# Order of the first attention's steps and of the gate constants in a two-layer kernel, one core

## The chip, the cores and the metric

The kernel runs on one core of a Trainium2 chip. It is one launch: every input is copied in from HBM, six blocks are computed one after the other, and the output is stored. The metric is the device time of one execution in microseconds (us). The engines of the core work through queues of their own, in the order in which the program wrote them, and wait for each other by semaphores: TensorE (PE), VectorE (DVE), ScalarE (ACT), GpSimd (POOL) and SyncE (SP), which here only issues DMAs.

## The reference

`x` is 4 x 128 tokens of width 128, `ctx` is 4 x 2048 x 128. Six blocks follow each other, each as `x = x + block(layernorm(x))`. The change touches the first and the fourth, and the hand-over from the first to the second.

```python
# block 1: cross attention with a mask; 16 heads of 8 channels
Q = heads(x @ Wq.T + bq); K = heads(ctx @ Wk.T + bk); V = heads(ctx @ Wv.T + bv)
scores = einsum('bhqd,bhkd->bhqk', Q, K) / sqrt(8)
scores = where((kidx - head) % 16 != 0, -inf, scores)     # head h sees keys h, h+16, ... : 128 keys
out = softmax(scores) @ V;  return out @ Wo.T + bo
# block 2: selective state space (x @ W_in, a causal convolution of 4 taps, silu, delta, scan, gate, W_out)
# block 3: SwiGLU with quantised weights and activations
# block 4: gated attention
gate = ctx @ Wg + bg
attn = softmax(einsum('bkd,bqd->bkq', gate, x), axis=1)    # over the 2048 keys
out = einsum('bkq,bkd->bqd', attn, ctx);  return out @ Wo + bo
# block 5: self attention with a relative bias; block 6: an 8-bit MLP
```

In block 4 the kernel never forms `gate`: it multiplies the queries by `Wg` ("gated queries", `g_T`) and adds, for each query, the product with `bg` (the gate constant, `c_gate`), which is one number per token. The softmax then needs a shift per token: minus the largest score of its row, with the constant taken in.

## The kernel before

**The tiling.** A batch is a tile of 128 tokens, there are four. In the first attention a head sees 128 keys, so a batch has 16 score tiles of 128 x 128; they are worked in four *groups* of four heads, one group to a PSUM bank (512 columns). Sixteen groups in all, numbered `w` or `t`.

**One group's way.** `scores` (PE): products of depth 32, since a group's four heads share a strip of 32 rows of `q_heads` and of the keys. `maximum_of` (DVE, L889): the row maxima from PSUM. `difference` (DVE, L897): scores minus maximum to `diff`. `turn_diff` (PE, L1402): four transposes back into the same bank. `exponentials` (ACT, L578): to `probs_T`, two batches deep.

**One batch's way.** `keys_values` (PE) and the copies of ACT (L550) give keys and values; `turn_values` (PE, L1345) turns the values and DVE (L843, `keys_values`) places them. `heads` (PE) multiplies the probabilities of four groups with the values, and with ones for the sums; `inverse` (ACT, L584 and L588) makes 1/sum; `scaled` (DVE, L884) gives `attn_T`; the projection (PE) goes to bank 5; `add` (DVE, L952) and `moments` give `x` and its statistics; `rsqrt_var` (ACT, L536), `normed` (DVE, L823), `turn_xn` (PE, L1316) and `copy_xn_T` (ACT, L544) give the turned, normalised input of block 2. Its convolution and gates are `channels(i, part)` on PE, by `SSM_GROUPS` (batches 0 and 1 together, then 2, then 3), then the product with `w_x` (`dbc_ps`), which the whole state-space block waits for.

**What sets the order.** Each engine has a loop over steps `t` (`attention(ph)`, ph 0 for the first attention, ph 1 for the self attention); a step's work is due at `t = stage + 4b` by the numbers in the line `VALUES, SCALE, ...`, the same for each batch. In phase 0 `scores` is called for every second `t` with two *strips* (two groups at a time, two banks), on a ring of five banks; in phase 1 it is called with four strips at once. The step `t` of PE is: scores, values, two `turn_diff`, `heads`, keys, projection, `turn_xn`, channels.

**Weights.** ACT makes sums of absolute weights at t = 6, 7, 8 (L605, the first waits for the DMA of `late_sb`); PE adds them up (`weight_sums`) in bank 7, DVE reads them (L853 to L855) at t = 10. The maxima of two more weights (L849), `pair_of_maxima`, `weight_maxima`, `spread_maxima` and `weight_inverses` stand at t = 16 to 22.

**Fills.** `keep_warm(n, bank)` is n matmuls of `ones` without a use, put where PE would stand still.

**The gated block.** Per batch: `turn_xn`, `copy_xn_T`, `gated_queries` (PE), `copy_g` (ACT, L731), four `gated_scores` of 512 keys, `maximum` (DVE, L1164), `shifts` (L1168 to L1171), the exponentials (ACT, L754, with `shift` as bias), transposes (L1723), copies (L1204), `mix`. The first batches run between the last steps of block 3: `turn_hidden` (L1631), its copy (L714) and `down` for batches 2 and 3.

## Time and profile before

| what | us |
|---|---|
| median of 3 runs (lowest, highest) | 236.3 (236.25, 237.12) |
| the profiled execution, its own time | 236.94 |
| its span, first to last instruction | 235.1 |
| PE busy / DVE busy / ACT busy / POOL busy in the span | 200.7 / 172.6 / 119.7 / 88.3 |
| mean granted TensorE clock | 0.977 |
| first attention and hand-over (first scores to the product that block 2 waits for) | 10.0 to 62.1 |
| block 2 and block 3 | 62.1 to 133 |
| gated block | 133 to 178 |
| self attention, MLP, store | 178 to 235.1 |

The time of a run is that of the whole execution, the span is what the profiler saw between its first and last instruction; 1.84 us lie around it. Times inside the profile count from the start of the span. The profiled execution lies within the runs shown, 0.64 above their median.

### The profile page before, as it was taken

The numbers are of one execution on the slowest core, as the hardware profiler recorded it, in microseconds if no ns is written. First come the engines' busy times: TensorE is split into PE (matmuls) and PEld (weight loads), VectorE is DVE, ScalarE is ACT, GpSimd is POOL, SyncE is SP. The second block draws the span as 40 slices with busy tenths as digits, with TensorE's granted clock in tenths as the row PEclk, the third lists the DMA queues.
The fourth block names the chain that finished last, engine by engine and source line by source line (L and its number), as shares of the span: only waits on it lengthen the run. The fifth ranks groups of instructions, "written<-read, shape, count | busy, mean of one in ns | idle before, by whom it ended". The sixth has DMA issues, their size and how long they took to land.

```text
span 235.1 us, 5061 instructions
## 1 busy us (share of the span) xinstructions
PE 200.7 (85%) x1868; PEld 141.3 (60%) x1868; DVE 172.6 (73%) x486; ACT 119.7 (51%) x292; POOL 88.3 (38%) x104
## 2 busy tenths in 40 slices
PE   8879998799997799999986679999988798876832
PEld 5568777688663245454463446867885776664421
DVE  2489485733399999999789879497775868816785
ACT  3343633435878897986065636335242344453431
POOL 7002408110047799998423064400002566522000
PEclk9999999999999999999999999999999999997696
DMA  6999950000079988300000001400000000000001
GB/s 213 389 427 409 418 242 4 3 0 0 8 216 377 233 96 96 56 1 0 0 3 0 0 0 50 133 0 3 0 0 3 0 4 3 3 3 3 0 0 45
DMA packets 9224, 20.23 MB, mean 86 GB/s; under 512 B 736, under 2 KB 5472, under 8 KB 8176
## 3 DMA queue, kind: packets, MB, share of 16 engines
q1 hardware_dynamic: 8912, 19.78, 27.2%
q8 instruction: 15, 0.25, 0.4%
q10 hardware_dynamic: 288, 0.13, 0.2%
q14 instruction: 9, 0.07, 0.1%
HBM read 17.52 MB, written 2.38 MB: 85 GB/s over the span
## 4 chain that ended last, share of the span: by engine, by line
PE 39%; POOL 17%; DVE 16%; issue 16%; ACT 7%; DMA 3%; SPq 1%; POOLq 0%; DVEq 0%; ACTq 0%
PE bank L1299 32%; POOL region L496 9%; POOL diff L520 6%; DMA ctx_T_sb<-ctx_T 3%; PE bank L1723 3%; PE bank L1402 2%; DVE diff L897 1%; DVE ext L1260 1%; DVE ext L1261 1%; DVE neg_max L889 1%; DVE region L1275 1%; PE bank L1316 1%; ACT region L676 1%; POOL region L485 1%; DVE region L1129 1%
## 5 line engine op out<-in xcount | busy, mean ns | idle before, releaser
L1054 DVE TENSOR_TENSOR_SCAN region<-region,bank 128x512 f32<-128x512 f32 x32 | 37.1, 1203 | 0.9 <-ACT region L690 0.8
L1299 PE MATMUL bank<-region,early_sb 128*128 128x512 f32 x64 | 33.8, 621 | 3.2 <-POOL region L496 2.1
L578 ACT ACTIVATE region<-bank 128x512 f32<-128x512 f32 x32 | 18.6, 594 | 21.7 <-PE bank L1402 21.5
L1299 PE MATMUL bank<-ones 128*128 128x256 bf16 x198 | 28.5, 300 | 1.1 <-POOL ones L432 1.0
L1299 PEld LDWEIGHTS bank<-ones 128*128 128x128 bf16 x198 | 20.6, 107 | 8.0 <-issue 2.2
L536 ACT ACTIVATE lnv<-mv,eps_col 128x1 f32<-128x1 f32 x24 | 7.0, 291 | 31.6 <-DVE mv L819 21.2
L690 ACT ACTIVATE region<-region,a_neg 128x508 f32<-128x508 f32 x32 | 21.1, 708 | 2.3 <-DVE region L1054 1.2
L1402 PE MATMUL bank<-early_sb,diff 128*128 128x128 f32 x128 | 18.8, 280 | 3.8 <-POOL diff L520 3.2
L1299 PE MATMUL bank<-ctx_T_sb,region 128*32 128x128 f32 (+1 forms) x160 | 20.7, 341 | 1.1 <-DMA ctx_T_sb<-ctx_T 0.7
L520 POOL TENSOR_TENSOR diff<-region,neg_max 128x512 f32<-128x512 f32 x15 | 15.5, 1044 | 12.4 <-DVE neg_max L908 12.4
L453 POOL TENSOR_TENSOR xb<-x,rows_sb 128x512 f32<-128x512 f32 x3 | 3.8, 1266 | 39.0 <-DVE x L1179 27.9
L1299 PEld LDWEIGHTS bank<-region,early_sb 128*128 128x128 f32 x64 | 9.8, 189 | 13.8 <-POOL region L496 13.0
L1402 PEld LDWEIGHTS bank<-early_sb,diff 128*128 128x128 f32 x128 | 14.0, 141 | 6.7 <-POOL diff L520 4.1
L908 DVE CUSTOM_DVE_ANT_0 region<-bank,region 128x128 f32<-128x128 f32 x64 | 14.4, 286 | 3.6 <-PE bank L1299 3.6
L1299 PE MATMUL bank<-k_T,region 32*128 32x128 f32 x256 | 15.1, 283 | 2.2 <-ACT k_T L550 1.0
L676 ACT ACTIVATE region<-region,b_tok 128x256 f32<-128x256 f32 x36 | 15.3, 495 | 2.5 <-PE bank L1576 2.5
L1299 PEld LDWEIGHTS bank<-region,ctx_sb 128*128 128x128 f32 x128 | 15.2, 192 | 1.9 <-issue 1.9
L1299 PEld LDWEIGHTS bank<-k_T,region 32*128 32x128 f32 x256 | 12.7, 186 | 5.3 <-ACT k_T L592 1.7
L1204 DVE COPY region<-bank 128x512 f32<-128x512 f32 x16 | 10.9, 686 | 6.6 <-PE bank L1723 6.5
L1299 PE MATMUL bank<-region,ctx_sb 128*128 128x128 f32 x128 | 15.6, 275 | 0.0
L1576 PEld LDWEIGHTS bank<-early_sb,region 128*128 128x128 f32 x72 | 9.0, 141 | 9.1 <-issue 8.1
L889 DVE TENSOR_REDUCE neg_max<-bank 128x4 f32<-128x512 f32 x16 | 10.3, 684 | 3.5 <-PE bank L1299 3.5
(234 smaller groups left out, 412.1 us busy)
## 6 DMA issues: line engine op xcount, KB each, us to landing
ctx_sb<-ctx SPq DMA_DIRECT2D x4, 1024.0 KB, 23.9
ctx_T_sb<-ctx_T SPq DMA_DIRECT2D x3, 1024.0 KB, 10.3
late_sb<-late SPq DMA_DIRECT2D x1, 2416.0 KB, 17.3
bias_scratch<-bias_vec SPq DMA_DIRECT2D x1, 2040.0 KB, 25.3
ctx_T_sb<-ctx_T SPq DMA_DIRECT2D x2, 512.0 KB, 5.9
diff<-c_scratch SPq DMA_DIRECT2D x4, 256.0 KB, 6.2
x<-c_scratch SPq DMA_DIRECT2D x4, 256.0 KB, 6.4
region<-bias_scratch SPq DMA_DIRECT2D x1, 1024.0 KB, 5.6
```

Source lines behind the costliest of these rows:

```text
L496: done(pool.tensor_tensor(read[:, k % 3, :], state[:, k % 3, :], c_rows(n), ALU.mult), "read")
L520: done(pool.tensor_tensor(diff[:, w % 4], neg_biased[:, t % 3], neg_max[:, w % 4, :, None].to_broadcast([P, HG, P]), ALU.subtract), "diff")
L578: done(act.activation(probs_T[:, w % (2 * NG)].rearrange("p h q -> p (h q)"), step_bank(w)[:, :], ACT.Exp, scale=1.0 if w < 16 else -1.0), ...
L676: ins = act.activation(du_B[:, i % 2, b].rearrange("p h c -> p (h c)"), du_T[:, b].rearrange("p h c -> p (h c)"), ACT.Copy, scale=b_tok[:, ...
L690: done(act.activation(dst, src, ACT.Exp, scale=a_neg[:, hf, n:n + 1]), "decay")
L889: done(dve.tensor_reduce(neg_max[:, w % 4, :], step_bank(w)[:, :].rearrange("p (h k) -> p h k", h=HG), AX, ALU.max, negate=True), "neg_max")
L908: ins = dve.tensor_tensor_reduce(neg_biased[:, t % 3, j, :], src[:, j, :], rel_bias[:, HG * g + j, :], -1.0, HIGHEST, ALU.add, ALU.min, ne ...
L1054: done(dve.tensor_tensor_scan(state[:, k % 3, :], decay[:, k % NDA, :], bank[3 + k % 3][:, :], 0.0, ALU.mult, ALU.add), "state")
L1204: done(dve.tensor_copy(p2_T[:, w % 4].rearrange("p c q -> p (c q)"), bank[4 + w % 2][:, :]), "p2T_sb")
L1299: return pe.matmul(dst, lhsT, rhs, start=start, stop=stop)
L1402: ins = pe.transpose(step_bank(w)[:, j * P:j * P + P], diff[:, w % 4, j, :], ident)
L1576: ins = pe.transpose(bank[3 + k % 3][:, b * P:b * P + P], du_B[:, BY_PE.index(n) % 2, b, hf, :], ident)
```

## The change

It has two parts.

**The first attention.** `scores` of phase 0 is called four times with four strips, once per batch: at t = 0, and then at t = 3, 7 and 11 behind `heads`. The ring of five banks gives way to a list of banks, and the wait on `probs_T_sb` is set so that two of the four groups' banks are free of older exponentials. A table `FIRST` gives for each step of a batch its own t in phase 0 (phase 1 keeps the old numbers). PE's loop ends at t = 17; the last `heads`, the last projection, the four `turn_xn` and all `channels` stand behind it in an order written out. The fills ahead of `heads` are left out for batches 2 and 3. The sums of weights move from bank 7 at t = 9 to bank 6 at t = 13 (PE) and from t = 10 to t = 15 (DVE); the maxima move behind DVE's loop. ACT's copies of the keys stand one step earlier, ahead of the exponentials of that step. The turned tiles of the first layer norm all go to bank 7, so that each `turn_xn` waits for the copy of the tile before; those of block 2's norm go to bank 6.

**The gated block.** The gate constants are made for batch 0 alone, for batch 1 alone, and for 2 and 3 together, where they were made by pairs. PE makes those of batch 0 ahead of the first scores, and turns batch 1 behind all four scores of batch 0 where it stood between the second and the third. DVE's `shifts` is a reduction with the sign turned and one operation with two steps, where it was a reduction and two operations.

On PE around the third batch's `heads` (names: `k_T` are scores, `diff` are `turn_diff`, `v_heads` and `ones_heads` are `heads`, `attn_T` the projection, `ones` a fill). Before:

```order
38 L1402 MATMUL bank<-early_sb,diff 128x128 x4
39 L1299 MATMUL bank<-cols_sb,attn_T 128x128
40 L1299 MATMUL bank<-k_T,region 128x128 x8
41 L1345 MATMUL bank<-early_sb,k_T 128x128 x2
42 L1402 MATMUL bank<-early_sb,diff 128x128 x8
43 L1299 MATMUL bank<-k_T,region 128x128 x8
44 L1402 MATMUL bank<-early_sb,diff 128x128 x4
45 L1299 MATMUL bank<-ones 128x256 x6
46 L1299 MATMUL bank<-region,v_heads 32x128 x16
```

On PE, the same place after:

```order
33 L1305 MATMUL bank<-k_T,region 128x128 x16
34 L1305 MATMUL bank<-cols_sb,attn_T 128x128
35 L1353 MATMUL bank<-early_sb,k_T 128x128 x2
36 L1410 MATMUL bank<-early_sb,diff 128x128 x8
37 L1305 MATMUL bank<-w_red,ones 128x3
38 L1305 MATMUL bank<-late_sb 16x256
39 L1410 MATMUL bank<-early_sb,diff 128x128 x4
40 L1305 MATMUL bank<-region,v_heads 32x128 x16
41 L1305 MATMUL bank<-region,ones_heads 32x128 x16
42 L1410 MATMUL bank<-early_sb,diff 128x128 x12
43 L1305 MATMUL bank<-cols_sb,attn_T 128x128
44 L1324 MATMUL bank<-early_sb,xn 128x128
```

All scores of batch 3 now stand ahead of the projection of batch 1 and of the last transposes, the sums of weights stand between them, the fill is gone, and three groups are turned behind `heads` of batch 2.

On PE at the hand-over (`region 128x256` and `128x128` are the convolutions, `region,late_sb` 256 or 128 wide are gates, 104 rows high is the product that block 2 waits for; `w_diag` is `spread_maxima`). Before:

```order
52 L1299 MATMUL bank<-region 128x256 x4
53 L1299 MATMUL bank<-ones 128x256 x6
54 L1299 MATMUL bank<-region,v_heads 32x128 x16
55 L1299 MATMUL bank<-region,ones_heads 32x128 x16
56 L1316 MATMUL bank<-early_sb,xn 128x128
57 L1299 MATMUL bank<-region 128x256 x4
58 L1299 MATMUL bank<-cols_sb,attn_T 128x128
59 L1299 MATMUL bank<-region,late_sb 128x256 x2
60 L1299 MATMUL bank<-region 128x128 x8
61 L1299 MATMUL bank<-region,late_sb 128x128 x2
```

On PE, the same place after:

```order
45 L1305 MATMUL bank<-region,v_heads 32x128 x16
46 L1305 MATMUL bank<-region,ones_heads 32x128 x16
47 L1324 MATMUL bank<-early_sb,xn 128x128
48 L1305 MATMUL bank<-region 128x256 x4
49 L1324 MATMUL bank<-early_sb,xn 128x128
50 L1305 MATMUL bank<-cols_sb,attn_T 128x128
51 L1305 MATMUL bank<-region 128x256 x4
52 L1324 MATMUL bank<-early_sb,xn 128x128
53 L1305 MATMUL bank<-region 128x128 x8
54 L1305 MATMUL bank<-region,late_sb 128x256 x2
55 L1305 MATMUL bank<-region,late_sb 128x128 x2
```

The first convolution, which stood ahead of the last `heads`, now stands behind it, and `spread_maxima`, once followed by eight convolutions and a gate, is now (four rows on, beyond this piece) the last thing ahead of the 104-high product.

On PE at the start of the gated block (`cols_sb,xn_T` are the gate constants, `ctx_T_sb` the scores, `ident_b` is `turn_hidden`). Before:

```order
140 L1316 MATMUL bank<-early_sb,xn 128x128
141 L1299 MATMUL bank<-xn_T,late_sb 128x128
142 L1299 MATMUL bank<-ctx_T_sb,region 128x512 x2
143 L1316 MATMUL bank<-early_sb,xn 128x128
144 L1299 MATMUL bank<-ctx_T_sb,region 128x512 x2
145 L1299 MATMUL bank<-xn_T,late_sb 128x128
146 L1299 MATMUL bank<-cols_sb,xn_T 128x1 x2
147 L1631 MATMUL bank<-ident_b,region 128x128 x4
```

On PE, the same place after:

```order
134 L1324 MATMUL bank<-early_sb,xn 128x128
135 L1305 MATMUL bank<-xn_T,late_sb 128x128
136 L1305 MATMUL bank<-cols_sb,xn_T 128x1
137 L1305 MATMUL bank<-ctx_T_sb,region 128x512 x4
138 L1324 MATMUL bank<-early_sb,xn 128x128
139 L1305 MATMUL bank<-xn_T,late_sb 128x128
140 L1305 MATMUL bank<-cols_sb,xn_T 128x1
141 L1650 MATMUL bank<-ident_b,region 128x128 x4
```

The transpose of batch 1, and all that follows from it, moved from the middle of the scores to their end.

The diff, cut to what the text speaks of:

```diff
-RING = 5
 VALUES, SCALE, PROJECT, ADD, RSTD, NORM, TURN = 6, 7, 7, 8, 8, 9, 10
 BY_HAND = 2
 
+FIRST_BANKS = (0, 1, 2, 3, 4, 7, 0, 1, 2, 3, 4, 7, 1, 0, 2, 3)
...
+FIRST = {"heads": {7: 0, 11: 1, 14: 2}, "inverse": {7: 0, 11: 1, 15: 2, 18: 3}, "scale": {7: 0, 11: 1, 15: 2, 19: 3},
+         "project": {7: 0, 11: 1, 17: 2}, "add": {8: 0, 12: 1, 16: 2, 20: 3}, "moments": {8: 0, 14: 1, 16: 2, 20: 3},
+         "rstd": {8: 0, 17: 1, 19: 2, 20: 3}, "norm": {9: 0, 15: 1, 19: 2, 21: 3}, "turned": {17: 0, 18: 1, 19: 2, 21: 3}}
...
+def batch_at(ph, t, what):
+
+    if ph == 0:
+        return FIRST[what].get(t)
+    b = due(t, LATER[what])
+    return b if b is None or what in ("heads", "inverse", "scale") or b < BY_HAND else None
...
-SSM_GROUPS = [(0, 2, [(1, 0), (1, 2 * P)], (0, 0)), (2, 3, [(2, 0), (2, P)], (2, 2 * P)),
+SSM_GROUPS = [(0, 2, [(1, 0), (1, 2 * P)], (0, 0)), (2, 3, [(2, 0), (2, P)], (7, 2 * P)),
...
-            at = bank[[7 - b % 2 * 4, 7, 5 + b % 2, 7 if b == 3 else b][n]]
+            at = bank[[7, 6, 5 + b % 2, 7 if b == 3 else b][n]]
...
-                    if ph == 0 and t % NG == 3 and t // NG + 1 < NB:
+                    if ph == 0 and t % NG == 2 and t // NG + 1 < NB:
...
-                    if ph == 0 and t == WEIGHTS + 4:
+                            token_extremes(batch_at(ph, t, "norm"))
+                    if ph == 0 and t == SUMS_READ:
                         weight_sums()
-                    if ph == 0 and WEIGHTS_REST <= t < WEIGHTS_REST + 2:
-                        reduce_weight(3 + t - WEIGHTS_REST)
-                    if ph == 0 and t == WEIGHTS_REST + 5:
-                        weight_maxima()
-                    if ph == 0 and t == WEIGHTS_REST + 6:
-                        weight_inverses()
...
+            reduce_weight(3)
+            reduce_weight(4)
+            weight_maxima()
+            weight_inverses()
...
-                link(dve.tensor_reduce(top[:, b:b + 1], row_max[:, b, :], AX, ALU.max))
-
-                link(dve.tensor_tensor(top_c[:, b:b + 1], top[:, b:b + 1], c_gate[:, b:b + 1], ALU.add))
-                done(dve.tensor_tensor(shift[:, b:b + 1], c_gate[:, b:b + 1], top_c[:, b:b + 1], ALU.subtract), "shift")
+                link(dve.tensor_reduce(top[:, b:b + 1], row_max[:, b, :], AX, ALU.max, negate=True))
+
+                done(dve.scalar_tensor_tensor(shift[:, b:b + 1], top[:, b:b + 1], c_gate[:, b:b + 1], c_gate[:, b:b + 1],
+                                              ALU.subtract, ALU.add), "shift")
...
-            token_steps(hid, h_abs, h_step, h_inv, h_mul, 1, "h_mul", [lambda: maximum(0, 0)])
+            token_steps(hid, h_abs, h_step, h_inv, h_mul, 1, "h_mul", [lambda: gate_columns(0, 1), lambda: maximum(0, 0)])
...
-            gate_columns(0)
             shifts(0)
+            gate_columns(1, 2)
...
+                elif n == 0 and b >= 1:
+                    pe.wait_ge(S["xnT_sb"], b)
...
-                if ph == 0:
-                    if b >= 1:
-                        pe.wait_ge(S["x_ready"], b)
+                if ph == 0 and b >= 1:
+                    pe.wait_ge(S["x_ready"], b)
+                if ph == 0 and b < NB // 2:
...
-                if ph == 0 and t >= RING - 1:
-                    pe.wait_ge(S["probs_T_sb"], t + 2 - RING)
+                if ph == 0 and b >= 1:
+
+                    pe.wait_ge(S["probs_T_sb"], t - 2)
+                    if b == 1:
+                        pe.wait_ge(S["v_sb"], 1)
...
             def attention(ph):
-                w_o = C("woT", 0, D) if ph == 0 else L("w_projT")
-                for t in range(STEPS[ph]):
-                    if ph == 0 and t < 4 * NB and t % 2 == 0 or ph == 1 and t in (NG, NG + 2):
+                for t in range(4 * NB + LAG if ph == 0 else STEPS[ph]):
+                    if ph == 1 and t in (NG, NG + 2):
                         scores(ph, t)
-                    elif ph == 1 and t == 0:
+                    elif t == 0:
...
+                    if ph == 0 and t in (NG - 1, 2 * NG - 1, 3 * NG - 1):
+                        scores(ph, t + 1, NG)
...
-            for part in (0, 1, "gates"):
-                channels(2, part)
+            turn_xn(1, 1, 0)
+            heads(0, NB - 1)
+            turn_xn(1, 1, 1)
+            channels(0, 0)
+            turn_xn(1, 1, 2)
+            project(0, NB - 1)
+            channels(0, 1)
+            turn_xn(1, 1, 3)
+            channels(1, 0)
+            channels(1, 1)
+            channels(0, "gates")
+            channels(1, "gates")
+            channels(2, 0)
+            pair_of_maxima()
+            channels(2, 1)
+            channels(2, "gates")
+            spread_maxima()
             for i, (b0, b1, _, _) in enumerate(SSM_GROUPS):
                 cols = slice(b0 * P, b1 * P)
...
-            pe.wait_ge(S["g_sb"], 1)
+            gate_columns(0, 1)
             for g in range(4):
                 gated_scores(0, g)
-                if g == 1:
-                    turn_xn(3, 2, 1)
+            pe.wait_ge(S["c_gate"], 1)
+            turn_xn(3, 2, 1)
             gated_queries(1)
-            gate_columns(0)
-            pe.wait_ge(S["g_sb"], 2)
+            gate_columns(1, 2)
             turn_hidden(2)
             down(2)
             for b in range(NB):
```

## Rows read from the trace of the kernel before

**Rows 1.** Stretches of the span: busy time of each engine, granted clock, DMA
```profile
core 0: us, PE busy (x) PEld busy (x) DVE busy (x) ACT busy (x) POOL busy (x), PEclk, DMA share, GB/s
34.00:46.00 12.00, 9.55 (x161) 7.70 (x154) 8.09 (x21) 5.02 (x15) 5.77 (x9) 1.00 0.02 4
145.00:178.00 33.00, 32.34 (x227) 26.58 (x225) 22.97 (x58) 12.94 (x43) 4.70 (x8) 1.00 0.12 33
211.00:215.00 4.00, 1.58 (x8) 0.83 (x7) 2.67 (x10) 2.87 (x8) 0.00 (x0) 0.90 0.00 0
215.00:221.00 6.00, 5.29 (x20) 3.00 (x21) 3.50 (x14) 1.33 (x3) 1.26 (x1) 0.50 0.01 3
```

**Rows 2.** Timeline, PE: scores with two strips, then with four (self attention)
```profile
9.99 1.16 PE L1299 MATMUL bank<-k_T,region 32*128 32x128 f32 x16
...
179.31 1.17 PE L1299 MATMUL bank<-k_T,region 32*128 32x128 f32 x32 [0.37 <-ACT k_T L592]
```

**Rows 3.** Timeline, batch 3: values turned, placed, two maxima, `x` of batch 1
```profile
37.80 0.44 PE L1345 MATMUL bank<-early_sb,k_T 128*128 128x128 f32 x2
...
38.27 0.35 DVE L843 TENSOR_TENSOR v_heads<-bank,v_bias 128x64 f32<-128x64 f32 x2 [2.40 <-PE bank L1345]
...
38.54 1.28 DVE L889 TENSOR_REDUCE neg_max<-bank 128x4 f32<-128x512 f32 x2
...
40.93 0.28 DVE L952 TENSOR_TENSOR x<-bank,xb 128x128 f32<-128x128 f32 x1
```

**Rows 4.** Timeline, ACT: the first sum of weights
```profile
23.43 0.63 ACT L605 ACTIVATE w_tmp<-late_sb 128x512 f32<-128x512 f32 x1 [0.54 <-DMA late_sb<-late]
```

**Rows 5.** Timeline, PE and ACT around `heads` of batch 2
```profile
42.23 1.07 ACT L578 ACTIVATE region<-bank 128x512 f32<-128x512 f32 x2
...
42.86 1.08 PE L1299 MATMUL bank<-region,v_heads 128*32 128x128 f32 x32 [0.69 <-ACT region L578]
...
44.88 0.28 ACT L584 ACTIVATE ln_sum<-bank 128x128 f32<-128x128 f32 x1 [1.59 <-PE bank L1299]
...
45.88 0.49 PE L1299 MATMUL bank<-cols_sb,attn_T 128*128 128x128 f32 x2 [0.37 <-DVE attn_T L884]
```

**Rows 6.** Timeline, the sums of weights on DVE and who waits
```profile
34.69 0.40 DVE L853 COPY bias_vec<-bank 16x256 f32<-16x256 f32 x1
...
35.52 0.30 PE L1316 MATMUL bank<-early_sb,xn 128*128 128x128 f32 x1 [0.66 <-DVE w_inv L855]
```

**Rows 7.** Timeline, the hand-over to block 2
```profile
47.08 1.89 PE L1299 MATMUL bank<-region 128*128 128x256 f32 x8
...
49.55 1.08 PE L1299 MATMUL bank<-region,v_heads 128*32 128x128 f32 x32
...
52.10 0.26 ACT L544 ACTIVATE region<-bank 128x128 f32<-128x128 f32 x1
...
57.55 0.38 PE L1299 MATMUL bank<-w_diag,ones 2*128 2x2 f32 x2 [0.51 <-DVE w_diag L860]
...
57.86 2.05 PE L1299 MATMUL bank<-region 128*128 128x128 f32 x16
...
58.16 0.17 DVE L865 RECIPROCAL w_inv<-w_scale 128x2 f32<-128x2 f32 x1
...
62.13 0.68 DVE L1014 COPY region<-bank 32x512 f32<-32x512 f32 x1 [3.80 <-PE bank L1299]
```

**Rows 8.** Timeline, the start of the gated block
```profile
132.97 0.33 PE L1316 MATMUL bank<-early_sb,xn 128*128 128x128 f32 x1 [0.47 <-DVE xn L823]
...
134.52 1.98 PE L1299 MATMUL bank<-ctx_T_sb,region 128*128 128x512 f32 x4 [0.37 <-ACT region L731]
...
137.73 1.49 POOL L509 TENSOR_SCALAR region<-region 128x512 bf16<-128x512 f32 x1
...
139.32 0.38 PE L1631 MATMUL bank<-ident_b,region 128*128 128x128 bf16 x4 [0.42 <-ACT region L731]
...
140.23 0.68 ACT L754 ACTIVATE region<-bank,shift 128x512 f32<-128x512 f32 x1
```

125 lines of the change are left out of this document (57 added, 68 removed).

## Prediction

> **What bounds the kernel now.** I read the chain of waits first, then the stretches, then the time line of the two places that the diff touches. The chain says that PE carries most of the span, but not what an edit of PE is worth: that depends on the stretch. In the first attention PE, DVE and ACT pass each batch around a ring. From 34 to 46 us PE is busy 9.55 of 12 us and DVE 8.09 [rows 1]: neither is full, so what counts is how soon the next piece is handed on. One place shows it: DVE stood idle for 2.40 us until the values of batch 3 were turned, at 38.27, although that is a step of 0.44 us on PE; PE came to it late because it goes through its queue in order [rows 3]. At the hand-over to block 2 the product that everything waits for is ready at 62.13 [rows 7]. In the gated block PE is busy 32.34 of 33 us from 145 to 178 [rows 1], so a delay ahead of 145 us stays to the end, and a saving on DVE behind it is hidden.
>
> **Four strips.** Two groups of scores take a row of 1.16 us; four groups, sixteen matmuls in place of eight, take 1.17 us where the self attention already does it [rows 2]. The matmuls of the four strips run beside each other, so eight calls of some 1.1 us become four: 4.4 us off PE's queue. Two fills are left out too; a fill costs nothing by itself as long as PE would have waited.
>
> That is no gain of 6 us, because DVE still has to take in the same groups. Two maxima and two differences take 2.39 us (38.54 to 40.93 in [rows 3]), eight times over. The Trainium skill says the same in "TensorEngine Tiling (Array Packing)", section "PSUM Bottleneck": tiling speeds up TensorE but not the emptying of PSUM, which may become the bound. By PE's rows alone the change would be worth 4.4 us, by that rule nearly nothing; the walk below lies between, since DVE also stood idle.
>
> **The walk through the first attention.** I follow the new queues with the distances between events in the rows of before. Two things hold it at the start. The first exponentials wait behind the turned scores as before, and ACT waits for the weights' DMA: the first sum starts at 23.43 whatever PE does [rows 4], 0.7 us with its read-out (0.63 and what lies behind). The sixth exponential now stands behind that sum and the seventh behind the second sum, while the new scores of batch 2 wait for the sixth. So those scores start at 24.8, the second sum ends at 25.35, the inverse of batch 0 starts there and its projection, 1.00 us later (44.88 to 45.88 in [rows 5]), at 26.35: no gain up to here, a loss of 0.4 us against PE's own readiness.
>
> From there a batch goes: projection; values turned 0.37 later and placed 0.47 after that (37.80 to 38.27), 0.27 to the maxima, 2.39 to the next piece of DVE [rows 3]; statistics, the layer norm's two small steps on ACT, and behind them in ACT's queue the last exponential that `heads` needs. That puts `heads` of batch 1 at 31.8; its projection is 3.02 us later (42.86 to 45.88 in [rows 5]), at 34.8. The values of batch 3 are placed at 35.7, maxima from 35.95, where before they started at 38.54: 2.6 us won. DVE adds `x` of batch 1 at 38.35, and `heads` of batch 2 starts at 38.7 in place of 42.86 [rows 5]: 4.2 us won.
>
> Now the new order takes its price. Groups 13 to 15 are turned behind this `heads`, at 40.6. The exponential of group 13 runs from 41.3 to 41.8, and only then the inverse of batch 2, 1.0 us later than `heads` would allow. Two exponentials (0.5 us each in sequence, 1.07 for two in [rows 5]) and the layer norm's two steps (0.4) follow; DVE normalises batch 1 at 43.9, makes the weights' scales in 0.83 us (34.69 to 35.52, where PE waited for it [rows 6]) and adds `x` of batch 2 at 45.0. The last `heads` waits for that: 45.4. Before it was at 49.55 [rows 7], so 4.15 us are won up to here.
>
> **The hand-over.** Before, it took 12.58 us from that `heads` to 62.13 [rows 7]. The new order adds to it: the first convolution, which lay ahead of `heads` (a row of 1.89, 1.75 without the overlap of its end [rows 7]); one more `turn_xn`, 0.15; a wait for the copy of batch 1, which stands behind the inverse in ACT's queue and so starts 2.55 us after `heads` (49.55 to 52.10) and ends at 2.8, while PE is through at 2.05: 0.8; and 0.1 for the last normalised tile. `spread_maxima` is now last: its result reaches `w_inv` 0.78 us after its start (57.55 to 58.16 and 0.17 on), PE would have gone on after 0.31 (57.86), and the product waits for it: 0.5. It takes away the wait of 0.51 ahead of `spread_maxima`. Sum: 1.75 + 0.15 + 0.8 + 0.1 + 0.5 - 0.5 = 2.8. So the first attention gives 4.15 - 2.8 = **1.3 us**. ACT's table load and the copies of the convolutions lie beside these steps and end before the product; if they don't, each costs its excess. POOL quantises the weights some 9 us later than before, in time it was idle in. Block 2 and 3 keep their length.
>
> **The gated block.** Before, batch 1 was turned between the second and third scores, and its copy lay under them. Now PE makes one constant (0.2, two passes of one column), then four scores of 0.9 each (1.98 for two in [rows 8]), and turns batch 1 at 134.52 + 0.2 + 3.55 = 138.25. From a `turn_xn` through copy, query and copy back to PE takes 132.97 to 134.52 = 1.55 [rows 8]: 139.8, and one constant more, 140.0. `turn_hidden` stands behind that; before it started at 139.32, held by POOL, whose row ends at 139.22 [rows 8]. The chain through ACT's copy to the first exponential (140.23) starts with it, so it moves by 0.65; with the same steps taken at their shortest 0.5, at their longest 0.9. I take **0.6 us lost**. The shorter `shifts` gains nothing here: the row of the first exponential has no idle time ahead of it, ACT was still copying [rows 8]. For later batches PE is full [rows 1], so one operation of DVE less is hidden; if PE stood idle there, it would be worth up to 0.2 each.
>
> **Sum.** 236.94 - 1.3 + 0.6 = 236.2 for the profiled execution. It lies 0.64 above the median, so the same step from the median gives 236.3 - 0.7 = **235.6**.
>
> **Rivals.**
> *The hand-over does not take it back.* Of the 4.15 us only the convolution that moved is paid (1.75) and the other waits (0.8, 0.1, 0.5) fall beside each other, and `turn_hidden` stays held by POOL alone: -2.4 + 0.1 gives 234.0. For it speaks that waits in one queue often overlap, against it that each of them has another releaser in turn.
> *The clock falls (slower).* Without the fills the walk leaves PE between 42.1 and 45.4 with three passes of work, and 0.85 us idle again at 47.4. Between 211 and 215 us PE was busy 1.58 of 4 us and the granted clock fell to half; it stayed at 0.50 from 215 to 221 [rows 1], that is at 1.2 GHz. The same here would run six microseconds, three of them at full speed's worth, through the last `heads` and the convolutions: 3 us less the 0.8 of waiting that it covers, so 235.6 + 2.2 = 237.8. It decides if the pause is as long as I walk it; the shorter pauses of before, 9.55 of 12 us busy from 34 to 46, left the clock at 1.00 [rows 1]. The Trainium skill, "TensorE: Matmul & The Clock Gate", Part 1, says that the slow clock is the default and activity releases it; the trace's fall at 215 agrees.
> *The start eats it.* The walk took the shortest hand-overs; if each of the four rounds costs 0.3 more than rows say, 1.3 us are gone and 0.6 stays lost: 236.9.
> *The strips do not run beside each other* with this bank list: four calls of 2.2 in place of 1.1, two of them ahead of a projection, 235.6 + 2.2 = 237.8. The rows of the self attention speak against it.
>
> **Chances.** The forecast 0.40 (own range 234.8 to 236.5), hand-over free 0.24, clock 0.20, start 0.11, strips 0.05. Half a per cent, about what a measurement of this kernel can tell, is 1.2 us: faster means under 235.1, slower over 237.5. Faster: 0.24 and 0.12 of the forecast's lower end, 0.36. Same: 0.28 + 0.11 = 0.39. Slower: 0.20 + 0.05 = 0.25. The range leaves out half of each of the outer ends: 233.6 to 238.0.
>
> **What the new profile would show.** Four rows of scores of 1.17 in the first 35 us; the second batch's projection near 34.8; `heads` of batch 2 near 38.7 and of batch 3 near 45.4; PE idle some 3 us between them; clock 1.00 there; the product's result on DVE at 60.8 in place of 62.13; block 2 and 3 of the same length; `turn_hidden` of batch 2 0.65 later against the first `turn_xn` of the block. I am wrong if the last `heads` comes later than 47.5, if the clock falls in that stretch, or if the gated block's first exponential comes no later after the block's start than the 7.26 us of before (132.97 to 140.23).

## The result

The changed kernel is slower, not faster: 238.76 us median of 20 runs against 237.08 of the kernel before on the same chips, ratio 1.0059 with the interval 1.0032 to 1.0087, about 1.4 us. I had forecast 235.6 with 233.6 to 238.0. Medians, here and below, are over all runs of a kernel; the ratios are taken against the kernel before on the same chip and leave out runs that lie over 1.5% above the fastest of their kernel. The profiled execution took 240.05 (before: 236.94), its span 238.3 (before: 235.1).

The page of the changed kernel, its first line and the granted clock by slices (40 slices of 5.96 us). Before, the clock row had its first digit under 9 at 211.6 us.

```profile
span 238.3 us, 5036 instructions
...
PEclk9999999959999999999999999999999999997696
```

The ninth digit, 47.7 to 53.6 us, is the 5: the slice that holds the end of the last `heads` and the first convolution. The stretches around it (columns as in [rows 1]):

```profile
43.00:46.00 3.00, 0.88 (x7) 0.56 (x11) 1.71 (x8) 1.51 (x6) 0.47 (x1) 1.00 0.00 0
46.00:49.00 3.00, 3.00 (x65) 2.52 (x64) 0.16 (x1) 0.35 (x2) 2.64 (x5) 0.63 0.02 5
49.00:52.00 3.00, 2.53 (x7) 1.89 (x7) 0.91 (x2) 0.96 (x5) 2.65 (x6) 0.50 0.00 0
52.00:55.00 3.00, 3.00 (x13) 2.48 (x12) 0.77 (x3) 0.46 (x2) 1.18 (x2) 0.73 0.00 0
```

PE is busy for 0.88 of the 3 us from 43 to 46, and then runs from 46.8 to 53.6 us at half speed, 1.2 GHz, although it is nearly full there (8.53 us of the 9 from 46 to 55). The steps of my walk on the timeline: the first scores, ACT's first sum [rows 4], the inverse of batch 0, the turn that waited ahead of the last `heads`, that `heads` [rows 7], `ones_heads` (the second half of `heads`), the first convolution, and the product on DVE [rows 7]:

```profile
9.33 1.17 PE L1305 MATMUL bank<-k_T,region 32*128 32x128 f32 x32
...
24.43 0.63 ACT L613 ACTIVATE w_tmp<-late_sb 128x512 f32<-128x512 f32 x1 [3.17 <-DMA late_sb<-late]
...
26.14 0.26 ACT L592 ACTIVATE ln_sum<-bank 128x128 f32<-128x128 f32 x1
...
45.57 0.30 PE L1324 MATMUL bank<-early_sb,xn 128*128 128x128 f32 x1 [1.65 <-DVE w_inv L863]
...
45.91 1.17 PE L1305 MATMUL bank<-region,v_heads 128*32 128x128 f32 x32
...
46.78 2.01 PE L1305 MATMUL bank<-region,ones_heads 128*32 128x128 f32 x32
...
49.67 3.78 PE L1305 MATMUL bank<-region 128*128 128x256 f32 x8 [0.47 <-ACT region L552]
...
64.34 0.68 DVE L1021 COPY region<-bank 32x512 f32<-32x512 f32 x1 [2.08 <-PE bank L1305]
```

The last `heads` comes 3.64 us earlier than before (49.55), the product 2.21 us later (62.13). Between them lie 18.43 us in place of 12.58. Two of PE's rows double: `ones_heads` 2.01 for 1.06, the convolution 3.78 for 1.89.

A second wait sits in this run beside the clock: the weights came late. Their DMA took 18.8 us from issue to landing, before 17.3, and in the new order ACT's first two sums hold up the inverse of batch 0. Before, that inverse waited another 0.82 us for PE when ACT was free, so there was room:

```profile
24.97 0.28 ACT L584 ACTIVATE ln_sum<-bank 128x128 f32<-128x128 f32 x1 [0.82 <-PE bank L1299]
```

The distance from the first scores (before 9.99 [rows 2]) tells the parts from each other. Before, the product comes 52.14 us behind them, and at 52.13 or 52.14 in the four experiments that keep the first attention of before (e2, f3, g2, g4), with first sums 13.20 to 13.76 behind the scores. In the changed first attention with the clock held (e1, g1, h1) it comes 50.26 to 50.60 behind them, so the order wins 1.5 to 1.9, and 37.23 to 37.25 behind ACT's first sum: it hangs on the weights. In this run it is 55.01. The first sum is 15.10 and the last `heads` 36.58 behind the first scores, where five other profiles of this order (e1, e3, g1, h1, h2) have 13.01 to 13.44 and 34.60 to 34.96: the late weights cost 1.6 to 2.0. So the first attention and its hand-over took 2.9 us more than before, some 1.5 won by the order, 2.7 lost by the clock and 1.7 by the weights; the first scores came 0.66 earlier, which leaves 2.21.

The start of the gated block, as [rows 8]:

```profile
135.19 0.33 PE L1324 MATMUL bank<-early_sb,xn 128*128 128x128 f32 x1 [0.47 <-DVE xn L831]
...
137.05 3.68 PE L1305 MATMUL bank<-ctx_T_sb,region 128*128 128x512 f32 x8
...
140.56 0.27 PE L1324 MATMUL bank<-early_sb,xn 128*128 128x128 f32 x1
...
143.28 0.68 ACT L762 ACTIVATE region<-bank,shift 128x512 f32<-128x512 f32 x1
```

Its first turn is 2.22 us later than before (132.97), just as the product is, so blocks 2 and 3 kept their length. Its first exponential is 8.09 us behind the turn, before 7.26: 0.83 us lost, where I had walked 0.65. The self attention's four-strip scores start 3.12 us later (182.43 for 179.31), and the span is 3.2 longer. So the profiled loss is 2.2 in the first attention and its hand-over and 0.85 in the gated block; nothing comes or goes behind it.

This profiled run is the second slowest of the changed kernel's twenty, with a mean clock, 0.963, that is their median; the late weights are a likely reason, but only profiled runs show when they came. In general the time goes with the clock. By mean granted clock, medians of all runs of the kernel before (the 116 beside the experiments), of the changed kernel (32, h2 below among them) and of the first attention's edit alone (24, e3 and h1 below):

| mean granted clock of the run | before | changed | first attention's edit alone |
|---|---|---|---|
| 0.973 and more | 236.46 (41 runs) | 237.06 (5) | 235.7 (5) |
| 0.966 to 0.972 | 237.32 (37) | 238.32 (8) | 236.8 (8) |
| 0.959 to 0.965 | 239.38 (10) | 239.06 (16) | 238.3 (2) |
| under 0.959 | 240.12 (28) | 240.44 (3) | 239.3 (9) |

At equal clock the first attention's edit alone gains in every row, 0.8 us in the first, where its five runs lie within 235.57 to 235.79. The changed kernel's five in that row spread from 236.07 to 238.63, so their median tells little: two of them are 0.3 under the median of before, the side on which order alone would put them (1.5 won, 0.83 lost), and what held the other three up is not shown; late weights are one candidate, which no experiment took out of this kernel by itself. The clock by itself does not make the whole difference either: 67% of the runs of before lie in the upper two rows and 41% of the changed kernel's, and the median clock is 0.969 against 0.963, but the average over all runs is 0.967 against 0.966, since before has more runs in the lowest row.

### The profile page after: what moved, and what is told of

Its sections match the earlier page's. It is cut to its first block, busy times and chain, and to the rows that moved or that the text cites. A ratio compares the mean times of both kernels' runs of the same rounds, so it can differ in the third digit from the quotient of the medians.

```text
span 238.3 us, 5036 instructions
## 1 busy us (share of the span) xinstructions
PE 198.9 (83%) x1856; PEld 138.6 (58%) x1856; DVE 172.1 (72%) x483; ACT 120.3 (50%) x292; POOL 88.2 (37%) x104
## 4 chain that ended last, share of the span: by engine, by line
PE 33%; POOL 17%; issue 16%; DVE 15%; DMA 8%; ACT 8%; SPq 2%; POOLq 0%; DVEq 0%; ACTq 0%
PE bank L1305 28%; POOL region L504 9%; DMA late_sb<-late 8%; POOL diff L528 6%; PE bank L1741 2%; DVE ext L1266 1%; DVE ext L1267 1%; DVE region L1281 1%; PE bank L1410 1%; PE bank L1324 1%; SPq L401 1%; ACT region L586 1%; ACT region L684 1%; ACT region L722 1%; POOL region L493 1%
## 5 line engine op out<-in xcount | busy, mean ns | idle before, releaser
L1305 PE MATMUL bank<-ones 128*128 128x256 bf16 x186 | 26.8, 302 | 1.0 <-POOL ones L440 1.0
L1305 PEld LDWEIGHTS bank<-ones 128*128 128x128 bf16 x186 | 19.5, 108 | 7.5 <-issue 1.8
L1305 PE MATMUL bank<-k_T,region 32*128 32x128 f32 x256 | 10.5, 282 | 3.7 <-ACT region L586 2.8
L1305 PEld LDWEIGHTS bank<-k_T,region 32*128 32x128 f32 x256 | 8.9, 186 | 5.8 <-issue 3.8
L1171 DVE TENSOR_REDUCE row_max<-bank 128x1 f32<-128x512 f32 x16 | 10.9, 688 | 1.8 <-PE bank L1305 1.6
## 6 DMA issues: line engine op xcount, KB each, us to landing
late_sb<-late SPq DMA_DIRECT2D x1, 2416.0 KB, 18.8
```

The lines of the kernel that those rows point to most:

```text
L1171: done(dve.tensor_reduce(row_max[:, b, g:g + 1], bank[g][:, :], AX, ALU.max), "row_max")
L1305: return pe.matmul(dst, lhsT, rhs, start=start, stop=stop)
```

## The experiments

### Is it the pause? e1 and e3

e1 fills the pause and changes nothing else.

```diff
                     if batch_at(ph, t, "project") is not None:
+                        if batch_at(ph, t, "project") == 2 and ph == 0:
+                            keep_warm(FILLS["pause"], 4)          # 7
                         project(ph, batch_at(ph, t, "project"))
+                        if batch_at(ph, t, "project") == 2 and ph == 0:
+                            keep_warm(FILLS["pause_rest"], 4)     # 14
```

> The changed kernel with two runs of fills on PE in the pause ahead of the last `heads` of the first attention: 7 ahead of the projection of batch 2, 14 behind it; nothing else. Theory A (the pause lets the granted clock fall, and that is the loss): the clock stays at 1.00 from 46 to 56 us, `ones_heads` takes 1.06 and the first convolution 1.89 again, the product's result comes to DVE at 61.3 instead of 64.34, and the kernel is about 2.5 us faster than the changed one, at 0.99 to 1.00 of the kernel before. Rival B (the new order of the hand-over costs the time, the clock only goes with it): the clock is back but the product comes no earlier than 63.5, the time stays within 0.7 us of the changed kernel. Rival C (fills keep PE from what is due): the last `heads` starts later than 46.5.

Measured: 238.21, ratio 1.0043 (1.0006 to 1.0079). The stretches of the pause and of the hand-over, then one of the gated block's start (columns as in [rows 1]); and the last `heads` and the product:

```profile
43.00:46.00 3.00, 2.84 (x50) 2.29 (x51) 1.58 (x7) 0.90 (x4) 1.17 (x2) 1.00 0.00 0
46.00:49.00 3.00, 2.37 (x46) 1.86 (x38) 0.92 (x2) 1.14 (x5) 2.65 (x5) 1.00 0.00 0
140.00:142.00 2.00, 1.94 (x9) 1.58 (x10) 1.03 (x4) 1.59 (x6) 0.31 (x1) 0.50 0.00 0
```

```profile
45.12 1.08 PE L1305 MATMUL bank<-region,v_heads 128*32 128x128 f32 x32
...
60.87 0.68 DVE L1021 COPY region<-bank 32x512 f32<-32x512 f32 x1 [2.08 <-PE bank L1305]
```

The mechanism is as theory A says: the clock stays at 1.00 over the hand-over, and from the last `heads` to the product it takes 15.75 us in place of 18.43. But the total is only 0.5 us better than the changed kernel's. In the profiled execution the clock fell at another place, 140 to 144 us, where the gated block starts. Theory A's 2.5 us were right for the stretch and wrong for the kernel.

e3 is the first attention's edit alone: the changed kernel with the gated stage's code of the kernel before.

> The changed kernel with the gated stage of the kernel before: the first attention's edit alone. Theory A (attention gains with the clock at full speed and loses it again through the clock): ratio to the kernel before 1.003 over its runs, product at 62 to 64.3 according to how long the clock is low. Rival B (the gated stage is the whole loss): ratio 0.997 to 1.000. The gated stage starts as late after the product as before, and its first exponential is 7.26 after its first turn.

Measured: 237.40, ratio 0.9992 (0.9948 to 1.0036). The stretches, and `ones_heads`, convolution and product (the last `heads` starts at 44.56):

```profile
43.00:46.00 3.00, 1.74 (x33) 1.61 (x37) 1.58 (x7) 0.37 (x2) 1.64 (x3) 0.79 0.02 5
46.00:49.00 3.00, 2.41 (x42) 1.83 (x34) 0.20 (x1) 0.82 (x4) 2.64 (x5) 0.64 0.00 0
```

```profile
46.10 2.00 PE L1307 MATMUL bank<-region,ones_heads 128*32 128x128 f32 x32
...
48.98 2.00 PE L1307 MATMUL bank<-region 128*128 128x256 f32 x8 [0.59 <-ACT region L553]
...
61.74 0.68 DVE L1022 COPY region<-bank 32x512 f32<-32x512 f32 x1 [2.08 <-PE bank L1307]
```

The clock fell here too, at 44.7 us, just as the last `heads` began, both halves of which took longer (1.83 and 2.00 for 1.08 and 1.06), but it was back after some 3 us, for the convolution (2.00, not 3.78). From `heads` to the product: 17.18, so the fall cost 1.5 and not 2.7, and the product came at 61.74, 0.4 ahead of before, but just as far behind the first scores (52.11, before 52.14): the fall ate what the order had won. Both theories had a part: the clock falls, and without the gated stage's edit the loss is gone.

### The gated stage: e2, f3, g4

e2 is the kernel before with the gated stage of the changed one, in three edits: constants batch by batch, batch 1 turned behind all four scores, shift in two operations.

> The kernel before with the gated stage of the changed one alone (constants batch by batch, batch 1 turned behind all four scores, shift in two operations). Theory A (my walk): first exponential of the gated stage 0.65 to 0.85 later against the first turn of the stage (8.1 instead of 7.26), the kernel 0.6 to 0.8 us slower, ratio 1.003. Rival B (a later batch takes it back, since PE waits for the shift somewhere): ratio 1.000.

Measured: 240.01, ratio 1.0070 (1.0018 to 1.0122). The first turn and the first exponential of the block, and two stretches:

```profile
133.02 0.33 PE L1314 MATMUL bank<-early_sb,xn 128*128 128x128 f32 x1 [0.47 <-DVE xn L822]
...
141.11 0.68 ACT L753 ACTIVATE region<-bank,shift 128x512 f32<-128x512 f32 x1
```

```profile
140.00:142.00 2.00, 1.23 (x11) 0.82 (x12) 0.18 (x2) 1.39 (x4) 1.51 (x2) 0.79 0.00 0
142.00:144.00 2.00, 2.00 (x6) 1.33 (x7) 1.52 (x4) 1.58 (x6) 0.00 (x0) 0.50 0.00 0
```

The distance to the first exponential is 8.09, exactly the changed kernel's; that the order costs 0.83 us is shown. In the profiled run the clock fell besides, from some 141 to 145, through the first transposes and the next batch's scores. By the ratios the parts add up: 1.0070 for this edit and 0.9992 for the first attention's (e3) make 1.0062, the changed kernel has 1.0059. So in the medians the loss comes with the gated stage, some 1.7 us, half of it order; that the other half is the clock is not shown, since before lost its clock in some runs too, and each interval is half a per cent wide either way. f3 adds fills there, and nothing else:

```diff
             turn_hidden(2)
+            keep_warm(FILLS["hidden_first"], 4)    # 8
             down(2)
+            keep_warm(FILLS["down_first"], 4)      # 2
```

> e2 (the kernel before with the gated stage of the changed one) with fills on PE around the first product of the hidden values: 8 ahead of it, 2 behind. In e2 the granted clock fell from 140.8 to 145 us in the profiled run, where PE waits for ACT twice; the order alone moved the first exponential by 0.83. Theory A (the loss of 1.007 is 0.83 us of order and the rest the clock): the clock stays at 1.00 from 138 to 148, the first exponential stays at 8.1 after the first turn, ratio to before 1.003. Rival B (the fills do not help, or the order alone costs 1.7 us): ratio 1.007.

Measured: 238.64, ratio 1.0057 (1.0018 to 1.0096). The clock stayed at 1.00 from 138 to 148 in the profiled run and the first exponential came 8.03 behind the turn, but the clock fell at 129 to 132 instead, ahead of the block. The ratio lies between the two theories and its interval holds both; it settles nothing by itself.

g4 is f3 with the one turn back in its old place, between the second and third scores:

```diff
             for g in range(4):
                 gated_scores(0, g)
+                if g == 1:
+                    turn_xn(3, 2, 1)
             pe.wait_ge(S["c_gate"], 1)
-            turn_xn(3, 2, 1)
             gated_queries(1)
```

> f3 (the kernel before, gated stage of the changed one, with its fills) with the turn of batch 1 back between the second and third scores; constants still made batch by batch, shift in two operations. Theory A (the 0.83 us come from that turn standing behind four scores): first exponential 7.26 to 7.5 after the first turn of the stage in place of 8.1; ratio to before 1.000 with the clock held. Rival B (the two additional constants and their waits cost it): still 7.9 or more.

Measured: 239.18, ratio 1.0028 (0.9974 to 1.0083), too wide to weigh half a microsecond. The same two rows:

```profile
133.76 0.33 PE L1314 MATMUL bank<-early_sb,xn 128*128 128x128 f32 x1 [0.47 <-DVE xn L822]
...
141.22 0.68 ACT L753 ACTIVATE region<-bank,shift 128x512 f32<-128x512 f32 x1
```

The trace answers what the time doesn't: 7.46 us to the first exponential, for f3's 8.03. So of the 0.83 us the turn behind four scores is some 0.6, and 0.2 is left for the constants made batch by batch. The two-operation shift is free and worth nothing: in g3 below, where it stands in the order of before, the first exponential comes 7.25 after the turn (130.16 to 137.41), before 7.26.

### What the four strips are worth: f1

f1 makes each four-strip call two calls of two strips again, in the changed order.

```diff
-                    pe.wait_ge(S["probs_T_sb"], t - 2)
+                    pe.wait_ge(S["probs_T_sb"], NG * b - 2)
...
+                    elif t == 0 and ph == 0:
+                        scores(ph, 0)
+                        scores(ph, 2)
...
                     if ph == 0 and t in (NG - 1, 2 * NG - 1, 3 * NG - 1):
-                        scores(ph, t + 1, NG)
+                        scores(ph, t + 1)
+                        scores(ph, t + 3)
```

> The changed kernel with every group of scores of the first attention made two strips at a time (eight calls of 1.16 in place of four of 1.17), the order otherwise that of the changed kernel. Theory A (DVE takes in the groups one by one and PE has idle time, so most of the 4.4 us is hidden): the first two maxima of each batch start on the first two strips as before, the last `heads` is at most 1 us later, time within 0.5% of the changed kernel, ratio to before 1.005 to 1.010. Rival B (PE's queue is what counts): 1.17 later per batch ahead of keys, values and projection, 3 to 4 us slower than the changed kernel, ratio 1.020.

Measured: 238.86, ratio 1.0095 (1.0053 to 1.0137). The profiled run had its clock at 1.00 up to 212 us, although its pause is as long as the changed kernel's (the turn's wait of 1.65). So its rows are full-speed rows: that turn, the last `heads` and the product.

```profile
46.73 0.30 PE L1324 MATMUL bank<-early_sb,xn 128*128 128x128 f32 x1 [1.65 <-DVE w_inv L863]
...
47.08 1.08 PE L1305 MATMUL bank<-region,v_heads 128*32 128x128 f32 x32
...
62.69 0.68 DVE L1021 COPY region<-bank 32x512 f32<-32x512 f32 x1 [2.08 <-PE bank L1305]
```

From ACT's first sum (23.88 here, 23.63 in e1) the last `heads` is 23.20 us away, in e1 21.49: 1.7 us later without the strips, of the 4.4 that PE's queue saves. Here the inverse of batch 0 no longer waits for the sums but for PE, so the first scores are the better start: from them it is 36.59, in e1 34.82 and in h1 34.60, 1.8 to 2.0 later. The product is 52.20 behind the first scores, before 52.14: without the strips the new order of the first attention gains nothing. Theory A had at most 1, B 3 to 4. The gain is neither all of PE's saving nor next to nothing; the measured price lies between the two.

### Closing the pause by order: e4, f2, f4

In the changed kernel the last `heads` waits for `x` of batch 2 at 45.34, and that stood on DVE behind the norm of batch 1 and the read-out of the weights' sums, which start at 44.48 and 44.74; the projection it needs was done at 43.92. e4 changes two numbers of the new tables:

```diff
-         "rstd": {8: 0, 17: 1, 19: 2, 20: 3}, "norm": {9: 0, 15: 1, 19: 2, 21: 3}, ...
+         "rstd": {8: 0, 17: 1, 19: 2, 20: 3}, "norm": {9: 0, 16: 1, 19: 2, 21: 3}, ...
-SUMS_READ = 15
+SUMS_READ = 14
```

> The changed kernel with two numbers of its order changed on DVE: the sums of the weights are read one step earlier (in DVE's idle time ahead of batch 2's heads), and `x` of batch 2 is added ahead of the norm of batch 1. No fills. Theory A (what matters is how long PE stands idle ahead of the last `heads`): the last `heads` starts at 44.4 instead of 45.91, the idle time between 43.9 and it nearly closes, the clock stays at 1.00 and the product comes at 59.8: 4 us faster than the changed kernel, ratio to the kernel before 0.987. Rival B (the clock falls in any case): heads at 44.4 but the clock at 0.50 for some 6 us after it, product at 62.8, ratio 1.000.

Measured: 236.84, ratio 0.9955 (0.9912 to 0.9998). The last `heads` and the product, and two stretches:

```profile
44.27 1.08 PE L1305 MATMUL bank<-region,v_heads 128*32 128x128 f32 x32 [0.43 <-DVE x L960]
...
59.88 0.68 DVE L1021 COPY region<-bank 32x512 f32<-32x512 f32 x1 [2.08 <-PE bank L1305]
```

```profile
43.00:46.00 3.00, 2.33 (x67) 2.08 (x67) 1.20 (x5) 1.40 (x5) 2.64 (x5) 1.00 0.02 5
182.00:185.00 3.00, 2.16 (x11) 2.16 (x12) 2.56 (x18) 1.11 (x4) 2.60 (x3) 0.66 0.00 0
```

Heads at 44.27 and product at 59.88, as walked (44.4 and 59.8), 4.5 us ahead of the changed kernel's profiled run and 2.25 ahead of before. Of the 4.5 us, 2.8 are the clock (15.61 from `heads` to the product for 18.43) and 1.6 the earlier `heads`. The edit shortens the pause without adding work, and the clock stayed up over the hand-over. The total gained 2 us and not 4: the clock fell at 183 us, where the self attention starts.

f2 also takes the wait for the weights' DMA out of the ring: ACT's three sums come two steps later (`WEIGHTS = 8` for 6).

> e4 (sums read one step earlier on DVE, `x` of batch 2 ahead of the norm of batch 1) and beside it ACT's three sums of the weights two steps later, behind the seventh exponential. In the changed kernel ACT stood 3.17 us for the weights' DMA with the sixth exponential and the inverse of batch 0 behind it, PE 1.84 and DVE 3.22 us. Theory A (that wait holds the whole ring): the inverse of batch 0 comes at about 24.0 in place of 26.14, the last `heads` at 42.5, the product 1.5 to 2 us earlier than in e4 (59.88), so 58.2, ratio to before 0.989. Rival B (the time comes back as a wait further on, for the maxima that DVE does in its own time): product at 59.5 or later, ratio 0.995 as e4. The clock may still fall at one of the pauses; then the time is 1 to 3 us above that.

Measured: 236.54, ratio 0.9953 (0.9916 to 0.9990). The inverse of batch 0 on ACT, the scores of batch 3, the product:

```profile
24.68 0.28 ACT L592 ACTIVATE ln_sum<-bank 128x128 f32<-128x128 f32 x1 [2.15 <-PE bank L1305]
...
33.81 1.17 PE L1305 MATMUL bank<-k_T,region 32*128 32x128 f32 x32 [0.84 <-ACT region L586]
...
59.51 0.68 DVE L1021 COPY region<-bank 32x512 f32<-32x512 f32 x1 [2.08 <-PE bank L1305]
```

The inverse of batch 0 comes 1.3 us earlier than in e4 (24.68 for 25.96), but the third sum (32.44) now stands ahead of the exponential that the scores of batch 3 wait for, and holds them by 0.84; the product is only 0.37 earlier, and 0.33 of that is an earlier start of the first scores (10.00 for 10.33). Rival B was right: the wait came back one batch later. What the edit does take away is the dependence on the weights: in f2, f4 and g3 the product comes 49.51 us behind the first scores each time, in f4 with weights that took 18.8 us to land.

f4 is f2 with the gated stage in the order of before, only the shift in two operations.

> f2 with the gated stage's order of the kernel before (both constants of a pair together, batch 1 turned between the scores), keeping only the shift in two operations. If the parts add: 0.8 us off f2 by the order, and the clock no longer falls at the start of the gated stage: ratio to before 0.985 (233.4). If the gated stage's order costs nothing once the first attention is earlier: as f2.

Measured: 234.78, ratio 0.9896 (0.9829 to 0.9963). Against f2 that is 1.8 us, more than the 0.8 of the order, from six runs; but in its profiled run the clock fell at 138 to 142 and at 182 to 190 all the same.

### Holding the clock everywhere: g1, g2, g3

The same fills (f3's, three and six ahead of the third and fourth token products of block 3, which the expectation calls the fourth, nine behind the first turns of the self attention) went into three kernels: the changed one (g1, with e1's fills too), the one before (g2), and f4 (g3).

> The changed kernel with fills on PE at every place where a profiled run so far has shown the granted clock fall: in the pause ahead of the last `heads` (7 and 14), around the third and fourth token products of the fourth block (3 and 6), around the first product of the gated stage's hidden values (8 and 2), behind the first turns of the self attention (9). Theory A (the change costs 0.83 us in the gated stage, gains 1.3 in the first attention, and loses the rest by the clock): clock at 1.00 up to 205 us, mean clock 0.978 in nearly all runs, ratio to before 0.998. Rival B (order costs more than I count): ratio 1.004 or more with the clock at 0.978.

Measured: 237.08, ratio 1.0014 (0.9978 to 1.0050). One stretch of the gated block's start, its four scores and its first exponential (the first turn starts at 130.82):

```profile
134.00:136.00 2.00, 2.00 (x4) 0.82 (x3) 1.06 (x4) 0.00 (x0) 0.54 (x1) 0.50 0.00 0
```

```profile
132.68 5.38 PE L1305 MATMUL bank<-ctx_T_sb,region 128*128 128x512 f32 x8
...
140.61 0.68 ACT L762 ACTIVATE region<-bank,shift 128x512 f32<-128x512 f32 x1
```

It got back 1.1 us of the 1.4, no more: the clock fell once more at a place without a fill, 133 to 137, and lay over the four gated scores: 5.38 us for 3.68, and 9.79 to the first exponential.

> The kernel before with the same fills except those in the first attention. It tells how much of the spread of the kernel before (235.9 to 242 us, mean clocks 0.979 to 0.946) is the same falls of the clock at these places. Theory A: mean clock 0.974 or more in nearly all runs, median 236.2 to 236.5, ratio 0.997 to 1.000, spread under 2 us. Rival B (the spread comes from elsewhere): mean clock still down to 0.947 in some runs, ratio 1.00.

Measured: 236.81, ratio 0.9968 (0.9932 to 1.0003). In eleven of twelve runs the mean clock was 0.968 or more and the time at most 238.13, the twelfth took 241.18 at 0.965; of the 29 runs of before beside it 18 had such a clock, and the highest took 242.52. So the fills take away most of the spread, which speaks for the same falls of the clock as its cause. The fills as such cost nothing that can be measured.

> f4 (sums read one step earlier, `x` of batch 2 first, ACT's sums two steps later, gated stage in the order of before with the shift in two operations) with these fills except those in the first attention. In f4's profiled run the clock fell at 138 to 142 and at 182 to 190. Theory A: those falls go, product at 58.7 to 59.5, mean clock 0.974 or more, median 233.6, ratio 0.987 or lower. Rival B (fills delay what is due, or the clock falls elsewhere): ratio 0.990 as f4.

Measured: 233.86, ratio 0.9852 (0.9804 to 0.9901), all six runs within 233.50 to 234.14. This is the best version of the study, 3.5 us under the kernel before beside it (237.41). Its mean clock is 0.968 to 0.973, under the 0.974 that I expected: it still falls behind 210 us. The clock by slices of 5.81 us:

```profile
span 232.3 us, 5086 instructions
...
PEclk9999999999999999999999999999999999996785
```

### Does the order hold its 1.3 us, and is the fall chance? h1, h2

h1 is e3 with e1's fills; h2 is the changed kernel again, beside it on one chip.

> The first attention's edit alone (gated stage of the kernel before) with the fills of e1 in the pause ahead of the last `heads`. Theory A (order worth 1.3 us, clock the rest): clock 1.00 from 40 to 62 us, product at 60.9, ratio to before 0.994 to 0.996. Rival B (the order is worth half a microsecond at most): product not ahead of before's by more than 0.6 once the start of the weights' sums is set equal, ratio 0.998 or more.

Measured: 238.13, ratio 1.0002 (0.9955 to 1.0049); most of its runs lost the clock elsewhere. Its profiled execution did not, and took 235.57. The stretch of the pause; then ACT's first sum, the last `heads` and the product:

```profile
43.00:46.00 3.00, 2.75 (x52) 2.22 (x53) 1.58 (x7) 0.69 (x4) 1.31 (x2) 1.00 0.00 0
```

```profile
23.41 0.63 ACT L614 ACTIVATE w_tmp<-late_sb 128x512 f32<-128x512 f32 x1 [1.08 <-DMA late_sb<-late]
...
45.00 1.08 PE L1307 MATMUL bank<-region,v_heads 128*32 128x128 f32 x32
...
60.66 0.68 DVE L1022 COPY region<-bank 32x512 f32<-32x512 f32 x1 [2.08 <-PE bank L1307]
```

The sum of weights starts at 23.41 as before (23.43), so start equals start: the product comes 1.47 earlier (1.88 counted from the first scores), and the execution took 1.37 less than the profiled one of before, at the same mean clock of 0.977. The median doesn't confirm it; this trace does, and the first row of the table.

> The changed kernel once more, beside h1 on one chip. If the fall of the clock ahead of the last `heads` is a matter of the order and not of chance, this profile shows it again between 44 and 54 us, the product at 63 to 64.5, ratio to before 1.006 and to h1 1.010 to 1.012 (0.8 us gated stage, 1.5 to 2 us clock). If it was chance, the clock is 1.00 there and the product comes at 61 to 61.5.

Measured: 238.63, ratio 1.0012 (0.9965 to 1.0059); the kernel before had a median of 238.32 beside it. Both forecasts of ratios were missed: 1.006 to before, and 1.010 to 1.012 to h1, which it equals within the noise (1.0012 and 1.0002). The loss of 0.59% is neither repeated nor ruled out. Three stretches, then the last `heads` and the product:

```profile
43.00:46.00 3.00, 1.31 (x30) 1.11 (x33) 1.58 (x7) 0.83 (x4) 1.24 (x2) 0.92 0.00 0
46.00:49.00 3.00, 2.74 (x45) 2.06 (x37) 0.00 (x0) 0.59 (x3) 2.61 (x5) 0.52 0.02 5
141.00:144.00 3.00, 2.83 (x10) 1.75 (x11) 1.52 (x4) 2.53 (x9) 0.41 (x1) 0.51 0.00 0
```

```profile
45.06 1.57 PE L1305 MATMUL bank<-region,v_heads 128*32 128x128 f32 x32
...
61.98 0.68 DVE L1021 COPY region<-bank 32x512 f32<-32x512 f32 x1 [2.08 <-PE bank L1305]
```

The fall is there again, some 3 us long as in e3, and costs 1.3 us (16.92 from `heads` to the product for h1's 15.66), so the product came at 61.98, ahead of the 63 to 64.5 expected for a fall; a second one lies over the gated block's start at 141 to 144. In the first profile of the changed kernel PE did the same work there and the clock stayed at 1.00. So of the four profiles that have the unfilled pause, with 1.65 us idle ahead of the turn, the fall came in three (the changed kernel twice, e3) and not in f1: likely, not certain. It costs 1.3 to 2.7 us by how long it lasts; at the gated block's start it comes in some executions and not in others. What decides that is open: the traces show the clock that was granted, not the reason.

## Why the prediction was wrong

**What bounds the kernel** held: delays ahead of 145 us stayed to the end (2.22 at the gated block's first turn, 3.05 at its first exponential, 3.2 in the span).

**The four strips.** Row of 1.17, as said. That the gain lies between nothing and 4.4 was right; with the order kept it is 1.7 to 2.0 (f1).

**The walk.** The wait for the weights' DMA is the first step that was off: 24.43 and not 23.43. That sum starts between 22.74 and 24.49 in the other profiles where it waits for the DMA, so 23.43 was a fair value and the profiled run an unlucky one. I had taken it as one fixed time and not as a risk: the old order had some room for a late landing (0.82 us ahead of the inverse), the new one has none, and it paid 1.6 to 2.0 us for it here. From there the distances hold: last `heads` 21.48 us behind the first sum, walked 21.97; the wait of ACT there was 3.17 and not 0.54, with the sixth exponential and the inverse behind it, as walked. Without the shift of 1.0 my 45.4 would have been half a microsecond too late.

**The hand-over.** Walked 15.4 (45.4 to 60.8). With the clock held e1 took 15.75, h1 15.66, e4 15.61. The sum of 2.8 was 0.2 to 0.35 too small. It came at 60.87 and 60.66 against my 60.8, so the attention's 1.3 us were right for an execution whose clock stays up (1.5 to 1.9 counted from the first scores).

**The gated block.** 0.65 forecast and 0.6 taken, 0.83 measured in the changed kernel and in e2: within my 0.5 to 0.9. The mechanism (the turn behind four scores) is shown by g4. That the shift gains nothing is shown by g3. But the ratio of e2 prices the whole edit at some 1.7 us; nothing in my walk stands for the other half.

**The step that failed** is the choice between the forecast and the rival of the clock: the sum has no term for a fall ahead of the last `heads`, and the fall came in three of four profiles with that pause and cost 1.3 to 2.7 us, which takes back the 1.3 us forecast there. I gave it 0.20 and wrote that it decides "if the pause is as long as I walk it". The pause was walked at 3 us with three passes of work, it came so (0.88 of 3 us busy), and my only row for such a pause was the fall at 211 to 221 [rows 1]. I held the shorter pauses of before against it, 9.55 of 12 us, which are of another kind: nothing in [rows 1] spoke for the clock to stay up. By my own rows the clock rival should have been the likeliest case. Its time, 237.8, lies 1 us under the measured median, and 0.8 of that is the base: I reckoned from 236.3, the median of three runs, and the twenty beside the changed kernel have 237.08. As ratios the forecast is 0.997, the rival 1.006, the measurement 1.0059. That this fits so well is in part luck: the rival has one fall of six microseconds and nothing for the gated block, the runs have shorter falls, at two places. "TensorE: Matmul & The Clock Gate" of the Trainium skill, Part 1, which I had cited for it, has the slow clock as the default that activity lifts; the trace agrees, 0.88 of 3 us busy and then 0.63 and 0.50, but f1 had the same pause and kept its clock.

**The price** I put at 2.2, from six slow microseconds less 0.8 of waiting. In the profiled run it was 18.43 - 15.7 = 2.7, in h2 1.3, in e3 1.5. So the size was fair too, for the stretch: what I had not seen is that it comes in two lengths, some 3 us and some 7.

**What I didn't see** is the second place. By the change the gated block's start has longer waits of PE on ACT (turn, copy, query, copy, constant, copy, all behind the four scores), and e1, e2, f2 and h2 show falls of the clock at 140 to 145 there, which no rival of mine named; the first profile of the changed kernel, e4 and f1 have the same order without fills and no fall. The order of before isn't safe either: f4 has it and fell at 138 to 142, while before, e3 and h1 didn't. So that the new order makes this fall likelier is not shown. A fall there lies ahead of a stretch in which PE is full [rows 1], so I expect it to stay to the end. The range ended at 238.0 because it counted one fall.

## What to carry to other kernels

Before a change that shortens a ring of engines, list for the bounding engine the stretches in which it will wait, old ones too, and put a number on what follows each at half the clock; if the change drops fills, or moves work out of a pause, take the fall as the likely case and not as the accident. Closing a pause by order (e4: two numbers, product 1.6 us earlier at equal clock, ratio 0.9955) beats filling it (e1: 1.0043). Before work is put behind a wait for a DMA, ask what a landing a microsecond later would hold up. With a spread like this one, half a microsecond is read from distances between rows at equal clock, counted from an event that the change doesn't touch, not from medians of twelve runs.
